# Moving the normalization of the rows from VectorE to GpSimd in a four-layer transformer kernel

## The reference

```
mu = jnp.mean(x, -1, keepdims=True)
var = jnp.mean((x - mu) ** 2, -1, keepdims=True)
return (x - mu) * jax.lax.rsqrt(var + EPS) * w + b
...
return _ln(x, lw, lb) * (1.0 + g) + bt
```

## Time and profile before

| what | value |
|---|---|
| three timed runs | 1691.32, 1695.45, 1696.75 us; median 1695.45 |
| the profiled execution | 1690.91 us, of which the span of its records 1688.9 us |
| busy: PE, DVE, ACT, POOL | 1518.5, 1403.1, 1095.0, 911.7 us |
| mean granted clock of TensorE, as a share of full speed | 0.97 |

### The profile page before, as it was taken

One profiled execution on the slowest core, in us unless ns is written; L12 is line 12 of the kernel. 1 busy time (PEld: TensorE's weight loads), 2 busy tenths in 40 slices (PEclk: granted clock), 3 DMA queues, 4 the chain that ended last, 5 costly groups with the idle time before them and its releaser, 6 DMA issues.

```text
span 1688.9 us, 40850 instructions
## 1 busy us (share of the span) xinstructions
PE 1518.5 (90%) x15228; PEld 1196.7 (71%) x15228; DVE 1403.1 (83%) x3745; ACT 1095.0 (65%) x4765; POOL 911.7 (54%) x1028
## 2 busy tenths in 40 slices
PE   6988999999889989999988989999989999989875
PEld 5876777677667777777766767776767778767653
DVE  5878788988997778898898868998898888888864
ACT  1766778657565777756576667766666686775632
POOL 3746454555765546455566646545575664554432
PEclk9999999999999999999999999999999999999975
DMA  9100000000000000000000000000000000000000
GB/s 328 37 1 2 2 2 2 7 4 4 7 8 2 2 1 2 2 7 7 6 3 7 2 2 2 2 7 1 7 7 7 2 2 2 2 2 3 3 1 3
DMA packets 14437, 20.91 MB, mean 12 GB/s; under 512 B 4064, under 2 KB 10784, under 8 KB 14240
## 3 DMA queue, kind: packets, MB, share of 16 engines
q1 hardware_dynamic: 14240, 18.31, 3.3%
HBM read 17.25 MB, written 1.05 MB: 11 GB/s over the span
## 4 chain that ended last, share of the span: by engine, by line
PE 47%; DVE 38%; POOL 8%; ACT 5%; issue 2%; DMA 0%; SPq 0%; POOLq 0%; ACTq 0%; DVEq 0%
DVE negmax L1007 9%; PE ps L665 9%; PE ps L691 6%; PE ps L552 6%; PE ps L704 5%; POOL E L859 5%; DVE E L1108 4%; ACT E L752 4%; DVE xn L967 3%; PE ps L678 3%; DVE E L1060 3%; PE ps L629 3%; PE ps L643 2%; PE ps L576 2%; PE ps L567 2%; PE ps L655 2%
## 5 line engine op out<-in xcount | busy, mean ns | idle before, releaser
L752 ACT ACTIVATE E<-ps,negmax 128x128 f32<-128x128 f32 x2048 | 719.3, 410 | 261.9 <-DVE negmax L1007 249.4
L859 POOL TENSOR_TENSOR E<-E,rinv 128x512 f32<-128x512 f32 x512 | 525.2, 1042 | 375.3 <-DVE rinv L1016 373.2
L752 ACT ACTIVATION_READ_ACCUMULATOR E<-ps,negmax 128x1 f32 x2048 | 509.7, 250 | 0.0
L1007 DVE TENSOR_REDUCE negmax<-ps 128x4 f32<-128x512 f32 x512 | 330.1, 680 | 59.3 <-PE ps L629 33.8
L665 PE MATMUL ps<-consts,E 128*128 128x128 f32 x2048 | 316.8, 285 | 39.7 <-POOL E L859 24.1
L1108 DVE COPY E<-ps 128x512 f32<-128x512 f32 x448 | 299.8, 678 | 54.6 <-PE ps L665 52.4
L665 PEld LDWEIGHTS ps<-consts,E 128*128 128x128 f32 x2048 | 233.0, 144 | 116.0 <-POOL E L859 67.6
L852 POOL TENSOR_TENSOR E<-E,prod 128x512 f32<-128x512 f32 x128 | 162.3, 1274 | 73.9 <-DVE prod L1063 72.2
L807 POOL TENSOR_TENSOR rstd<-ve,consts 128x1 f32<-128x1 f32 (+1 forms) x192 | 107.9, 563 | 83.5 <-DVE ve L960 74.0
L691 PE MATMUL ps<-E,VV 128*64 128x128 f32 x2048 | 139.4, 282 | 2.2 <-DVE E L1108 2.1
L761 ACT ACTIVATE VV<-ps 128x512 f32<-128x512 f32 x128 | 77.3, 671 | 89.8 <-PE ps L567 89.5
(11 more groups left out here) (130 smaller groups left out, 2757.1 us busy)
## 6 DMA issues: line engine op xcount, KB each, us to landing
w_f<-res_f SPq DMA_DIRECT2D x6, 256.0 KB, 11.5
qT<-in_x SPq DMA_DIRECT2D x16, 64.0 KB, 1.8
w_wq<-res_wq SPq DMA_DIRECT2D x2, 512.0 KB, 7.8
w_wk<-res_wk SPq DMA_DIRECT2D x2, 512.0 KB, 8.4
w_wv<-res_wv SPq DMA_DIRECT2D x2, 512.0 KB, 9.1
w_wo<-res_wo SPq DMA_DIRECT2D x2, 512.0 KB, 9.8
w_cq<-res_cq SPq DMA_DIRECT2D x2, 512.0 KB, 10.8
w_co<-res_co SPq DMA_DIRECT2D x2, 512.0 KB, 13.7
```

The costliest lines, as they stand in the source:

```text
L752: last = nc.scalar.activation(E[p][:, h, :], bank(u, j * N, (j + 1) * N), ACT.Exp, bias=negmax[p][:, h:h + 1], accum_out=sums[p][:, h:h + 1])
L859: tt(e, e, rinv[p][:, T4 * g:T4 * g + T4].unsqueeze(2).broadcast_to([N, T4, N]), ALU.mult).then_inc(done[POOL], 1)
L1007: nc.vector.tensor_reduce(negmax[p][:, T4 * g:T4 * g + T4], bank(u).rearrange("p (h m) -> p h m", h=T4), AX, ALU.max, negate=True).then_in ...
```

## The change

GpSimd gets the `norm` step, right behind its own `power` in the list of steps, with planned durations of 0.45 us (0.8 in block 0) where VectorE's had 0.25 (0.5). The instructions are the same tensor_scalar operations with the same operands, issued on GpSimd, after a wait for GpSimd's own count of `power`. TensorE's `T` waits for GpSimd's count in place of VectorE's. In the last block the step that the `sum` follows is GpSimd's `norm`. Nothing else is edited, but the planner runs with the new list, so the orders of all four engines and the banks are planned anew.

```diff
     add(POOL, "power", 0.56, (DVE, "aggr"))
+    add(POOL, "norm", 0.45 if b else 0.8, (POOL, "power"))
...
-    add(DVE, "norm", 0.25 if b else 0.5, (POOL, "power"))
-    add(PE, "T", 0.14, (DVE, "norm"), fills=("T",))
+    add(PE, "T", 0.14, (POOL, "norm"), fills=("T",))
     add(DVE, "T", 0.32, (PE, "T"), *([] if b else [(POOL, "xb")]), empties="T")
-    total = (POOL, "xb") if OUT_ROW[b] is not None else (DVE, "norm")
+    total = (POOL, "xb") if OUT_ROW[b] is not None else (POOL, "norm")
...
                 if step == "T":
-                    count = DONE[DVE, "norm", b, s]
-                    if fresh(pe, done[DVE], count):
-                        pe.wait_ge(done[DVE], count)
+                    count = DONE[POOL, "norm", b, s]
+                    if fresh(pe, done[POOL], count):
+                        pe.wait_ge(done[POOL], count)
...
-            tt = nc.gpsimd.tensor_tensor
+            tt, ts = nc.gpsimd.tensor_tensor, nc.gpsimd.tensor_scalar
...
+                elif step == "norm":
+                    count = DONE[POOL, "power", b, s]
+                    if fresh(pool, done[POOL], count):
+                        pool.wait_ge(done[POOL], count)
+                    src = X[p][:, :] if b else xin[p]
+                    last = ts(xn[p][:, :], src, mv[p][:, 0, 0:1], rstd[p][:, 0:1], ALU.subtract, ALU.mult)
+                    if b == 0:
+                        last = ts(cn[p][:, :], cin[p], mv[p][:, 1, 0:1], rstd[p][:, 1:2], ALU.subtract, ALU.mult)
+                    last.then_inc(done[POOL], 1)
...
-                elif step == "norm":
-                    count = DONE[POOL, "power", b, s]
-                    if fresh(dve, done[POOL], count):
-                        dve.wait_ge(done[POOL], count)
-                    src = X[p][:, :] if b else xin[p]
-                    last = ts(xn[p][:, :], src, mv[p][:, 0, 0:1], rstd[p][:, 0:1], ALU.subtract, ALU.mult)
-                    if b == 0:
-                        last = ts(cn[p][:, :], cin[p], mv[p][:, 1, 0:1], rstd[p][:, 1:2], ALU.subtract, ALU.mult)
-                    last.then_inc(done[DVE], 1)
```

## The result

The changed kernel took 1707.89 us in the median of four runs (1705.46 to 1709.87), the kernel before 1695.64 (1691.32 to 1696.75): a ratio of 1.0076, 95% interval [1.0054, 1.0099]. It is slower by 0.76%, some 13 us, where 1671 us had been forecast and 1706 was the end of the range. The profiled execution took 1706.82 us.

A forecast was written before the change was run, and what follows sets the result against it. TensorE and VectorE, in turn, were taken to bound the kernel. Terms of -48.0, -6.1, +8 and +14.3 us summed to -31.8; two thirds kept, -21, led to 1671 us, range 1640 to 1706.

The forecast's parts named there:

- GpSimd's queue: On the chain, other GpSimd steps delayed by 96.6 us more work: 0.148 us a microsecond, +14.3 us.
- the length of the norm: One norm of 128 columns on GpSimd: 0.47 us, between 0.26 and 1.27, nearest row a two-tensor addition of 458 ns.
- two thirds: Share kept, as a choice, of the -31.8 us sum because TensorE's chain is close behind: -21 us.
- What bounds the kernel: TensorE, 90% of the span, and VectorE, 83%, set the end in turn; GpSimd, at 54%, has room.
- VectorE's relief: On the chain, -48.0 us of VectorE's queue, and 15.8 us go in 19 stretches where the transpose was next.
- VectorE's busy time: VectorE loses the norms' 111.4 us of its 1403.1, some 71 of it work and 40 waits for GpSimd.
- The norm behind another step: In GpSimd's queue between power and norm, a 1.04 us multiplication stands in 0.4 of 19 stretches: +8 us.
- Rival (c): Slower: GpSimd's queue gates every block, seen at line 511's wait; 1716 us; without queueing, norms above 1.1 us; chance 0.22.
- GpSimd's wait for itself: Between power and norm on GpSimd: 0.03 us, taken from VectorE; 6 us of idle time left out.
- The new orders: A planner figure nearer to the forecast norm should keep the order better, no number; 9 us in the range for replanning.
- The signs I had named: VectorE near 1292 us, GpSimd near 1008, TensorE idle 20 less, line 511 waiting at most 41; chain: VectorE down, GpSimd up.
- Rival (b): Nothing gained: TensorE's own work sets the pace and VectorE's freed time is idle; 1691 to 1696 us; chance 0.16.

The follow-up runs named there:

- e7: Kernel before, same orders, VectorE's norms compute one column only, the others keep older values: 1653.04 us, ratio 0.9783.
- e11: e7 plus, behind each GpSimd power, a dummy tensor_scalar of the norm's form (two in block 0) that no other engine waits for: 1716.01 us, ratio 1.0148.
- e2: Norm moved to GpSimd right behind its power, all other steps in the orders of the kernel before: 1724.11 us, ratio 1.0180.
- e4: Kernel before, same orders, VectorE's norms compute 16 of the 128 (96) columns only: 1685.43 us, ratio 0.9948.
- h2: Kernel before, same orders; GpSimd waits for VectorE's norm before its next step where planned within 0.12 us of power (56 norms): 1688.60 us, ratio 0.9991.
- h3: Kernel before, same orders; GpSimd waits for VectorE's norm before its next step where planned within 0.45 us of power (108 norms): 1691.41 us, ratio 1.0009.
- e3: Changed kernel, same orders, GpSimd's norms compute 16 of the 128 (96) columns only: 1683.11 us, ratio 0.9941.
- e6: e2 with GpSimd's norms computing 16 of the 128 (96) columns only: 1680.46 us, ratio 0.9944.
- e5: Kernel before, planner told 0.5 us (1.0 in block 0) for VectorE's norm in place of 0.25 (0.5), orders redrawn: 1720.98 us, ratio 1.0179.
- e12: Kernel before, planner told 0.34 us (0.66 in block 0) for VectorE's norm, a second redraw of the orders: 1721.25 us, ratio 1.0170.
- e1: Changed kernel, planner told 0.8 us (1.48 in block 0) for GpSimd's norm in place of 0.45 (0.8): 1716.04 us, ratio 1.0127.

## Why the prediction was wrong

In per cent of the kernel before, with its orders kept: the relief of VectorE by e7 gives 2.17, GpSimd's load takes 3.65 (e11), the norm's own way through GpSimd less the rest of the relief 0.32 (e2), together +1.80; the changed kernel's own orders are 1.04 better, together +0.76.

The step that failed is the price of GpSimd's queue. With it the length of the norm was mis-sized, but by itself that does not explain the miss: at the forecast's own prices 0.80 us in place of 0.47 adds (0.80 - 0.47) x (0.148 x 208 + 19) = 16.4 us, two thirds of it 11, and 1671 becomes 1682, still a gain, where 1708 was measured. By the steps of the forecast:

- **What bounds the kernel**: two full engines, in turn. Right as far as it went; the third engine, at 54%, was taken at its share of the chain of that time, 8%, and got 20% with 163 us more.
- **VectorE's relief**, -48.0 and most of -15.8 at full value, two thirds of it kept, about -42: about right. e7 gave 37 with roughly half of the busy time gone, so the whole may be worth more. That it is mostly queue and waits for GpSimd and not work is borne out by e4 against e7; h2 and h3 took such waits away only at GpSimd's expense, so it isn't shown that the waits can be had back for nothing.
- **VectorE's busy time**, 111.4 us less: 79.7 measured. Here the forecast took the sum of the instructions' lengths for busy time. The lengths of all VectorE groups add up to 1594.5 us before and 1487.9 after, 106.6 less, so other instructions take a net 4.8 us longer now (line 998 alone 4.0). The other 27 us are overlap of the records, which busy time counts once: the norm of the earlier trace rows runs from 506.29 to 507.34, and the view has VectorE's next instruction start before its end:

```profile
507.26 0.68 DVE L1108 COPY E<-ps 128x512 f32<-128x512 f32 x1
```

- **The length of the norm**, 0.47 us between 0.26 and 1.27: mis-sized, 0.80 measured. The nearest row was an addition with two inputs. Two operations with a scalar each cost 3.2 ns a column, and 0.39 us for none (e3).
The line-rate sentence of the Trainium skill's "GPSIMD Engine Reference", section "Engine selection", gave an estimate of 0.37 and was further off; the trace does not agree with it for this form.
- **GpSimd's queue**, 0.148 us for a microsecond, +14.3: this is the step that failed. It took GpSimd's share of the chain (8%) over its work as the price of more work, and then kept two thirds of this cost too, where the reason given for the two thirds speaks of gains alone. e11 measured 61.7 us for 164.5 us, 0.38 for one; from 0.44 to 0.80 us a norm the price was 0.54 in the orders of before (e2 against e6), 0.33 in those of the changed kernel (e3). A share of the chain says nothing of the steps just beside the chain. My account of the rest, argued from the orders and the waits: with fixed orders every step behind an inserted one is later by its length, as long as no idle time in between takes it up, and TensorE, in order too, waits for the first late one: in e2 GpSimd stood waiting for the variance in front of 56 of its 192 powers, before it was 82, so its queue ran dry less often.
- **The norm behind another step**: right, and about right in size as far as the list tells; what each place costs was not measured. In the changed kernel's list 117 of 192 norms have another step between them and `power`, but only 75 have a multiplication there, 0.39 of them, where I took 0.4; some have several, 94 multiplications in all. Line 511 waits less than before all the same. Rival (c) had the right engine and sign, but put the place wrong: not the wait of line 511 but that of the probabilities, in a kernel with the orders of before (49.3 us against 24.1). Its point of decision, a norm of 1.1 us, was too high: e3 and the changed kernel lie on either side of the kernel before, at 0.44 and 0.80.
- **GpSimd's wait for itself**, 0.03 us: 0.10 measured, 20 us of idle time in front of the norms in e2, which I had left out with 6.
- **The new orders**: I gave them no number and 9 us in the range. Two redraws of the same instructions moved the time by 29 and 30 us (e5, e12), so the forecast of a single redrawn kernel had luck in it either way. My remark that a plan with truer figures would be kept better did not hold in any of three tries (e1, e5, e12).
- **The signs I had named**: TensorE's idle time was to fall by 20 us and rose by 6.9. Line 511 was to wait not over 41 us, and VectorE's share of the chain to fall and GpSimd's to rise; these held, in a kernel that is slower, so they could not tell. None of the signs looked at TensorE's wait for the probabilities.
- **Rival (b)** was nearer in size, but its reason, that TensorE sets the pace, does not hold here. Relief of VectorE is worth 37 us, and TensorE was busy for 91.8% of the middle before and 92.8% in e7. What eats it is GpSimd's own load: e11, where VectorE's busy time grew by 5.8 us only. The sentence of the Trainium skill's "Perfetto Trace Analysis", section "Optimizing Scalar/DVE Operations", that offloading between the two engines might not help came true in outcome; the sharing that it gives as the reason is not what took the gain back here, by the same 5.8 us.

## What to carry to other kernels

An engine with 45% idle time in a static in-order schedule is not free: add a dummy of the planned length that nobody waits for, and look at that time before moving real work there. In this kernel a share of the chain priced taking work off an engine fairly well and putting work on it far too low. Where a planner draws the order anew with each edit, keep the old order in one experiment, or the edit and the draw can't be told apart. Add up busy time from an engine's records only with their overlap in mind.

## What the runs showed of the hardware

GpSimd's tensor_scalar with two operations and two per-row scalars takes 0.80 us for 128 columns, 0.44 for 16, and 0.61 for 128 with one operation and one scalar. Where GpSimd waits for its own last instruction, the next starts 0.10 us after that one's end (e2), on VectorE 0.03 us. VectorE's tensor_scalar from and to the rows' memory takes up to 1318 and 1262 ns with 128 and with 16 columns beside a busy GpSimd, and 277 at most with one. VectorE's records overlap: an instruction behind a norm can start 0.08 us before its end. ScalarE's Identity with scale and bias took 0.50 us for 128 columns.
